# The last sample's y round three PSUM buffers, evicted by two engines and stored chunk by chunk, and d of a narrow tile over whole columns

## What is computed

```python
# layer 0 (im is relu(x) as channels by all pixels)
mn = mean(im); p = clip(u.T @ (im - mn), -cv, cv)
q = round((p - dmin) * scale) / scale + dmin      # 255 levels, min and max over all samples
x = u @ q - mean(u @ q) + mn
# layer 1
out = relu(bn(w_conv1 @ x))                       # 256 channels: z, h in the kernel
d = relu(bn(w_dr @ out + b_dr))                   # 128 channels: d, g in the kernel
cov = (d - mean(d)) @ (d - mean(d)).T / M         # M = 56*56 = 3136
r = sum_h(w_row * bn(cov)) + b_row
att = sigmoid(w_fc @ r + b_fc)                    # one number for each channel and sample
return x * att                                    # y in the kernel
```

## Time and profile before

| | before |
|---|---|
| median of 3 runs | 1895.87 us |
| lowest and highest | 1895.66 and 1897.51 us |
| profiled execution, its own time | 1896.12 us |
| its span | 1894.3 us |
| PE, ACT, DVE busy over the span | 88%, 79%, 81% |
| DMA, mean over the span | 252 GB/s |

### The profile page before, as it was taken

One profiled execution on the slowest core, in us unless ns is written; L12 is line 12 of the kernel. 1 busy time (PEld: TensorE's weight loads), 2 busy tenths in 40 slices (PEclk: granted clock), 3 DMA queues, 4 the chain that ended last, 5 costly groups with the idle time before them and its releaser, 6 DMA issues.

```text
span 1894.3 us, 39985 instructions
## 1 busy us (share of the span) xinstructions
PE 1673.7 (88%) x13394; PEld 1316.6 (70%) x13394; DVE 1533.0 (81%) x2806; ACT 1496.7 (79%) x2272; POOL 460.1 (24%) x136
## 2 busy tenths in 40 slices
PE   8999999999992000699999999999999999999998
PEld 8999999999991000467666666666666766666664
DVE  6888888888887755667888888888888888888883
ACT  6777777777769997678888878788788788887876
POOL 6888888888860000000000000000000000000000
PEclk9999999999995555799999999999999999999999
DMA  9998999999999999402545546455464464554634
GB/s 332 373 375 305 372 360 322 371 342 339 376 349 405 430 430 430 158 1 124 183 158 212 187 153 233 165 189 199 163 222 170 172 222 156 212 186 153 234 113 204
DMA packets 139775, 477.37 MB, mean 252 GB/s; under 512 B 10576, under 2 KB 33232, under 8 KB 124752
## 3 DMA queue, kind: packets, MB, share of 16 engines
q1 hardware_dynamic: 139728, 476.75, 68.3%
HBM read 284.04 MB, written 192.68 MB: 252 GB/s over the span
## 4 chain that ended last, share of the span: by engine, by line
PE 56%; ACT 1%; DVE 1%; issue 1%; ACTq 0%; DVEq 0%
PE y_ps L909 18%; PE z_ps L935 17%; PE d_ps L885 14%; PE cov_ps L866 5%; PE ch_ps L920 1%; ACT h L980 0%; PE ch_ps L898 0%; PE ch_ps L897 0%; ACT hh L985 0%; DVE g L1130 0%; PE cov_ps L869 0%; ACT p_res L1008 0%; DVE hl L1121 0%; PE cov_ps L841 0%; ACT gg L972 0%
## 5 line engine op out<-in xcount | busy, mean ns | idle before, releaser
L299 POOL TENSOR_TENSOR xl<-early,xh 128x1568 fp32r<-128x1568 f32 x128 | 459.2, 3588 | 97.5 <-ACT xh L258 97.5
L1121 DVE TENSOR_TENSOR hl<-h,hh 128x1024 f16<-128x1024 f32 (+2 forms) x224 | 244.1, 1090 | 99.3 <-ACT hh L985 99.0
L909 PE MATMUL y_ps<-qr,udh 128*128 128x512 f16 (+2 forms) x896 | 313.5, 353 | 4.0 <-ACT p_res L1008 3.6
L935 PE MATMUL z_ps<-qr,wl 128*128 128x512 f16 (+2 forms) x896 | 314.2, 354 | 0.0
L935 PE MATMUL z_ps<-qr,wh 128*128 128x512 f16 (+2 forms) x896 | 313.9, 353 | 0.0
L909 PE MATMUL y_ps<-qr,udl 128*128 128x512 f16 (+2 forms) x896 | 313.0, 352 | 0.0
L1008 ACT ACTIVATE p_res<-y_ps,att_cy 128x512 f32<-128x512 f32 (+2 forms) x448 | 298.2, 713 | 9.5 <-PE y_ps L909 4.5
L258 ACT ACTIVATE xh<-early 128x1568 fp32r<-128x1568 f32 x128 | 194.1, 1517 | 140.0 <-PE pp L316 139.9
L980 ACT ACTIVATE h<-z_ps,sb_h 128x512 f32<-128x512 f32 (+2 forms) x448 | 264.5, 627 | 25.7 <-PE z_ps L935 21.9
L885 PE MATMUL d_ps<-vh,hh 128*128 128x128 f16 (+1 forms) x1600 | 282.3, 220 | 1.6 <-DVE hl L1121 1.6
L885 PE MATMUL d_ps<-vh,hl 128*128 128x128 f16 (+1 forms) x1600 | 281.6, 219 | 0.0
(11 more groups left out here) (172 smaller groups left out, 2817.4 us busy)
## 6 DMA issues: line engine op xcount, KB each, us to landing
early<-in_x_dram SPq DMA_DIRECT2D x128, 784.0 KB, 6.8
out_dram<-p_res SPq DMA_DIRECT2D x31, 3136.0 KB, 10.2
early<-p_scratch SPq DMA_DIRECT2D x42, 1568.0 KB, 12.7
p_res<-p_scratch SPq DMA_DIRECT2D x112, 512.0 KB, 4.2
p_scratch<-early SPq DMA_DIRECT2D x56, 784.0 KB, 7.8
p_scratch<-late SPq DMA_DIRECT2D x56, 784.0 KB, 7.8
p_res<-p_scratch SPq DMA_DIRECT2D x56, 384.0 KB, 3.2
late_tile<-p_scratch SPq DMA_DIRECT2D x13, 1568.0 KB, 12.8
```

Source lines behind the costliest of these rows:

```text
L299: nc.gpsimd.tensor_tensor(xl[:, k % 2], xs[:, k], xh[:, k % 2].bitcast(F32), ALU.subtract).then_inc(split_done, 1)
L909: last = nc.tensor.matmul(y_ps[:, m, 0:widths[c]], part[:, k, m * P:(m + 1) * P], qr[:, slot, k, columns(c)], start=k == 0 and part is udh ...
L935: last = nc.tensor.matmul(z_ps[:, m, 0:w], part[:, k, m * P:(m + 1) * P], qr[:, a, k, columns(s)], start=k == 0 and part is wh, stop=k == ...
L1121: nc.vector.tensor_tensor(hl[:, par, :, 0:w], h32[:, par, :, 0:w], hh[:, par, :, 0:w], ALU.subtract).then_inc(h_split, 1)
```

## The change

Five things are changed, all in the third block.

1. `reduced` gives the narrow tile 128 columns of `hh` and `hl` instead of 64. The 64 columns more hold what an earlier chunk left there; their results land in 64 PSUM partitions that nothing uses. This holds for all 32 samples.
2. In the phases without a sample of their own, PE issues y ahead of the covariance at s = 1 and ahead of spread at s = 2.
3. The last sample's y goes round `y_ps`, `z_ps` and `d_ps`, which are no longer needed (`final_output`). PE issues chunks 0, 1 and 2 in one piece at s = 4, ahead of the logits, and then a chunk in each step.
4. The last sample's y is evicted by two engines, half 0 by ACT and half 1 by DVE, each with a semaphore of its own, `half_free0` and `half_free1`.
5. The last sample is stored in seven pieces, one for each chunk, and each waits for both halves.

```diff
+            FINAL = CH * (N - 1)
+            def final(o):
+                return isinstance(o, int) and o >= FINAL
+            final_ps = [y_ps, z_ps, d_ps.rearrange("p m g c -> p m (g c)")]
...
-                    sp.wait_ge(y_free, K + K * (CH * n + end))
+                    if final(CH * n if isinstance(n, int) else None):
+                        for m in range(K):
+                            sp.wait_ge(half_free[m], end)
+                    else:
+                        sp.wait_ge(y_free, K + K * (CH * n + end))
...
-                last_parts = [(0, 3), (3, 5), (5, 6), (6, CH)]
+                last_parts = [(c, c + 1) for c in range(CH)]
...
-                            q = min(P, widths[c] - t * P)
-                            parts = [(hx[:, par, k, t * P:t * P + q], vx[:, k])
+                            parts = [(hx[:, par, k, t * P:(t + 1) * P], vx[:, k])
                                      for k in range(K) for hx, vx in ((hh, vh), (hh, vl), (hl, vh))]
                             for n, (lhs, rhs) in enumerate(parts):
-                                last = nc.tensor.matmul(d_ps[0:q, par, t], lhs, rhs, start=n == 0,
+                                last = nc.tensor.matmul(d_ps[:, par, t], lhs, rhs, start=n == 0,
...
+                def final_output(o, c):
+                    buf = final_ps[c % 3]
+                    if c == 1:
+                        pe.wait_ge(z_read, K * CH * N)
+                    if c == 2:
+                        pe.wait_ge(d_read, CH * N)
+                    for m in range(K):
+                        if c == 0:
+                            pe.wait_ge(y_free, K * o + m + 1)
+                        if c >= 3:
+                            pe.wait_ge(half_free[m], c - 2)
+                        for k in range(K):
+                            for part in (udh, udl):
+                                last = nc.tensor.matmul(
+                                    buf[:, m, 0:widths[c]], part[:, k, m * P:(m + 1) * P],
+                                    qr[:, (N - 1) % 2, k, columns(c)],
+                                    start=k == 0 and part is udh, stop=k == K - 1 and part is udl)
+                        last.then_inc(y_done, 1)
...
+                        if final(o):
+                            for n in range(0, 3) if c == 0 else range(c + 2, min(c + 3, CH)):
+                                final_output(FINAL + n, n)
+                            return
...
-                        if s == 1:
+                        if exists(r2, a):
+                            if s == 1:
+                                covariance(r2, a, s)
+                            spread(r2, a, s)
+                        outputs(r2, a, s)
+                        if s == 1 and not exists(r2, a):
                             covariance(r2, a, s)
-                        spread(r2, a, s)
-                        outputs(r2, a, s)
+                        if not exists(r2, a):
+                            spread(r2, a, s)
...
+                            if final(o):
+                                act.wait_ge(y_done, K * (o) + 1)
+                                nc.scalar.activation(yo[:, slot, 0, columns(c)], final_ps[c % 3][:, 0, 0:widths[c]],
+                                                     ACT.Identity, scale=att_cy[:, 0, 0:1],
+                                                     bias=att_cy[:, 0, 1:2]).then_inc(half_free[0], 1)
+                                continue
...
+                            if c == 0:
+                                dve.wait_ge(attb_done, N)
+                                dve.wait_ge(out_stored[slot], 16 * (N // 2))
+                            dve.wait_ge(y_done, K * (o) + 2)
+                            nc.vector.tensor_scalar(yo[:, slot, 1, columns(c)], final_ps[c % 3][:, 1, 0:widths[c]],
+                                                    att_cy[:, 1, 0:1], att_cy[:, 1, 1:2], ALU.mult,
+                                                    ALU.add).then_inc(half_free[1], 1)
```

More of the change, by code:

```diff
@@ L720, in layer_kernel @@
         y_done, y_free = sem("y_done"), sem("y_free")
+        half_free = [sem(f"half_free{m}") for m in range(K)]
         with ExitStack() as c_:
@@ L1122, in phase @@
                                                     ALU.subtract).then_inc(h_split, 1)
+                        if has(r2, a, s, CH + Y_LAG) and final(output_chunk(r2, a, s)[0]):
+                            o, slot, c = output_chunk(r2, a, s)
+                            if c == 0:
[5 more added lines that the diff above has]
+                                                    ALU.add).then_inc(half_free[1], 1)
                         if has(r2, a, s, 1):
```

## The result

| | before | after |
|---|---|---|
| median of 9 runs each | 1897.48 us | 1891.24 us |
| lowest and highest | 1895.32 and 1898.49 us | 1890.02 and 1893.39 us |
| profiled execution, its span | 1896.12 us, 1894.3 us | 1892.99 us, 1891.2 us |
| ratio after to before, 95% interval | | 0.9971, 0.9962 to 0.9979 |

The account below looks back on a forecast made before the run. PE was taken to bound the steady part and the last two samples' transfers the end; 6.9 us (narrow tile) plus 2.4 us (tail) off 1895.87 us gave 1886.6 us, range 1885.2 to 1889.3 us.

Parts of the forecast that it names:

- What bounds the middle: Steady part of the third block: PE wholly busy, other engines with some 13% slack, so PE time freed is kernel time.
- The narrow tile: Border of d and covariance: the narrow shape costs 0.215 us a sample, 6.9 us over 32 samples.
- the narrow tile gives nothing: Rival at the narrow tile: another engine makes the gaps or takes up the freed time; 1893.5 us, chance 0.05.
- Sample 30 earlier: At the end, y of chunk 4 fills PE's idle 1.30 us, so sample 30's store is issued 1.55 us earlier.
- the logits later: Last sample: the logits wait behind three chunks of y, so evictions start 1.9 us later, hidden under sample 30's flow.
- two engines: Last y: ACT and DVE evict halves side by side, 0.73 and 0.69 us per 512 columns.
- The hole in the flow: DMA between the last two samples' stores: 0.85 us of almost no flow, counted as time to gain.
- the tail gives nothing: Rival at the end: later attention or small rows in the stores eat the 2.4 us; 1889.0 us, chance 0.14.
- The slower rival: SP's queue at the end: seven stores run one behind the other, 3.0 us fixed each; 1904.8 us, chance 0.03.
- The granted clock: PE without pauses: a granted clock falling under 0.988 would make the kernel slower; chance 0.01.
- The size: Whole kernel: 6.9 us from the narrow tile and 2.4 from the tail, 9.3 us less, from a median of 1895.87.

Follow-up runs that it names:

- e4: Changed kernel with the covariance of chunk 6 issued between the two halves of y at s = 1; ratio to before 0.9956.
- e1: Kernel before with only the narrow tile of d widened to whole columns (part 1 of the change); ratio to before 0.9978.
- e2: Changed kernel with the narrow tile as before, so parts 2 to 5 alone; ratio to before 0.9998.
- e3: Changed kernel with the logits behind chunk 1 of the last y instead of behind chunk 2; ratio to before 0.9964.
- e6: Changed kernel with the moves of e3 and e4 together; ratio to before 0.9956.
- e8: e3 with the last sample stored in four pieces instead of seven; ratio to before 0.9965.
- e7: e6 with sample 30 stored in three pieces (chunks 0 to 3, 4 and 5, 6); 1883.9 us, ratio to before 0.9935.
- e11: Changed kernel with sample 30 stored in three pieces and nothing else changed; ratio to before 0.9960.
- e9: Changed kernel unchanged, profiled a second time; ratio to before 0.9966.
- e10: Changed kernel with DVE's g of chunk 6 put ahead of its hl of chunk 0 at s = 0; ratio to before 0.9987.

## Why the prediction was wrong

- **What bounds the middle.** "In the steady part every 0.1 us that PE's stream loses is 0.1 us of the kernel, and the other engines have some 13% of slack": the second half is the step that failed, and with it the sum's term of 6.9 us, taken whole "since PE is wholly busy there"; 4.4 came. A share of busy time says nothing of the slack of one chain. The chain from z of chunk 0 over h, hh, hl, g and gg to the covariance of chunk 6 had some 0.1 to 0.18 us to spare (0.215 freed, 0.03 to 0.12 given back), and PE's waits on gg, 2.4 us in 11 samples, stood in the list that I cited for its longest row only.
- **The narrow tile.** Its price was right: 6.9 forecast, 6.8 in e4. The changed kernel keeps 4.4 of it. The Trainium skill, page "TensorEngine Tiling (Array Packing)", section "Key Properties", says that a change of tiling mode drains TensorE; the trace fits it, with about 0.1 us more at each of the two changes, gone in e1, but it does not show a drain as such. The 64-row tile of the covariance still has two such changes in each sample.
- **The rival "the narrow tile gives nothing"** named the right mechanism, another engine that takes up the time freed, and got 0.05. It came in part, and the forecast had no case for a part.
- **Sample 30 earlier, the logits later, two engines.** 1.7 us earlier against 1.55, 1.87 later against 1.9, DVE's eviction 0.81 us with a pitch of 0.72 against 0.69: these terms held.
- **The hole in the flow** is the second step that failed. The end was forecast as 1.55 + 0.85. Only the 1.55 was there (e2: 1.4, e4: 1.6). The span ends 18.7 to 19.5 us after sample 30's store issue in the ten profiles that store it whole, while y ends up to 3.4 us apart; I had counted 18.0, with the 0.85 as idle. It was idle for fourteen of sixteen shares of that store; the last one landed 2.0 us behind these, and from there the 8.0 us to the end of the span run without a hole. The changed kernel's 1.0 is then 1.7 from the earlier issue, less 0.4 for a landing of 11.2 instead of 10.8 us, less 0.2 for seven pieces. Why that landing varies by 0.8 us between profiles stays open.
- **The rival "the tail gives nothing"** had 0.14. The end gave less than half of its 2.4, but neither by the later attention (e3, e6: 1.7 us of compute change nothing) nor, but for 0.2 us, by small rows in the stores (e8).
- **The slower rival**, seven stores one behind the other, is excluded by e7's single flow and by e8. Its fixed part of 3.0 us was read from stores that landed in a full queue: with sample 30 out of the way the last 320 KB landed 2.2 us after their issue (e11), of which the bytes need 0.8 at 408 GB/s.
- **The granted clock.** I named a fall below 0.988 in the steady part as a mishap; behind the fall near 812 us, which before has too, it stayed at 1.00. It fell where I had not looked, behind the stop for the attention. There it puts the last eviction 18.8 us behind the last covariance, where e2 and e4, with the same last y and no fall, have 17.15: 1.7 us of compute. It cost the changed kernel little or nothing, as the transfers ended later; where they are off the path, e11 was forecast at 20.7 without and 22 with it, and measured 21.6.
- **The size.** The profiles' 4.4 and 1.0 us agree with the 5.5 us of the ratio; the forecast had 6.9 and 2.4. Of the 4.6 us between 1886.6 and the measured median, 1.6 are the median of before, which was 1895.87 us over three runs and is 1897.48 over nine.

## What to carry to other kernels

Before an engine's freed time is counted as the kernel's, look at the short waits of that engine too, and ask for each whether its releaser will also come earlier; here 0.215 us a sample were freed and up to 0.12 came back at the next wait. A stationary tile of another shape in a stream of whole ones costs its two borders, so let it compute rubbish over the full width where the results land in unused partitions. At the end of a kernel, count from the landing of the last large store and not from the last eviction or from the full flow's end, and cut the store before the last one as well.

## What the runs showed of the hardware

- At the start of the third block, after 133 us of idle time, the granted clock was 0.50 and rose to 1.00 at moments some 5 us apart in executions of one program. From the first z to the first covariance this made 13.6 us (after) and 11.3 us (e9). It is not the only cause of the scatter of 3 us between runs: in e2, e6 and e8 the first covariance is late (787.9 to 789.0 us) with an early rise, since the third block began 2.2 to 4.0 us later than in the others.
- A stop of PE of 1.83 us was followed by a fall to 1.2 GHz for 3.4 us in four of eight executions, at the end. One of 2.20 to 2.21 us, at the first covariance of chunk 6, was followed by such a fall in eleven of eleven, and one of 1.07 us at that place (e10) by none.
- A store's issue on SP took 0.37 us with little under way, and up to 1.30 us behind a store of 3136 KB.
- Of the sixteen landing records of a store of 3136 KB the last came 1.3 to 2.4 us behind the fifteenth, in all ten profiles that have that store at the end; in e3, 25 GB/s flowed in the last 2 us. Stores issued while it is under way end with the same lag; where 1.0 and 2.3 us lay between its landing and the next issue, the last store had none (e7, e11). Why, stays open.
